# A clear between two scatters of the key phase, and statistics last in the normalized projections of a GNN kernel

## The reference, cut to what matters

```
h = max(layernorm(x), 0); x = x + GAT(h, 3 rounds, 1 head)      # L0
h = max(layernorm(x), 0); x = x + RGCN(h, 4 bases, edge types)  # L1
h = max(layernorm(x), 0); x = x + GAT(h, 1 round, 8 heads)      # L2
h = max(layernorm(x), 0); x = x + edge_conv(h)                  # L3
```

## Time and profile before

| | |
|---|---|
| median of three runs | 3939.06 us |
| profiled execution | 3923.35 us, its span 3921.4 us |
| busy: TensorE, DVE, ACT, POOL | 58%, 58%, 41%, 55% of the span |
| key phase | to 271 us, POOL's scatters from 57.4 to 187 us |
| p0 | first statistics 1310.2 us, last residual ends at 1456.4 us |
| p4 | first statistics 2649.2 us, last residual ends at 2864.3 us |

### The profile page before, as it was taken

The page is one execution under the profiler, slowest core; times in us unless marked ns, Lnnn a source line. Parts: engine busy times, 40 slices in busy tenths (PEclk is TensorE's granted clock), DMA queues, the critical chain, the costliest instruction groups (busy, mean ns, idle before and its releaser), DMA issues. The chain is left out here.

```text
span 3921.4 us, 53964 instructions
## 1 busy us (share of the span) xinstructions
PE 2263.7 (58%) x12833; PEld 1777.4 (45%) x12833; DVE 2282.0 (58%) x8009; ACT 1610.7 (41%) x3565; POOL 2157.8 (55%) x2121
## 2 busy tenths in 40 slices
PE   1035899999898565465565567754526443344333
PEld 1023676676677554364464444434425332233222
DVE  4154999999898785334345378866575333333233
ACT  0005999999997573223323322324411222122100
POOL 3618765575564332581185255546500588888755
PEclk9998999999999786577577588887756666666665
DMA  2140122332231454651663733333304333333253
GB/s 64 27 181 20 44 90 87 100 103 87 87 92 39 133 157 116 161 139 42 186 174 87 203 95 99 87 98 81 90 16 118 109 74 64 75 74 65 51 145 117
DMA packets 569029, 380.48 MB, mean 97 GB/s; under 512 B 51389, under 2 KB 511942, under 8 KB 568386
## 3 DMA queue, kind: packets, MB, share of 16 engines
q1 hardware_dynamic: 510050, 329.99, 28.7%
q0 software_dynamic: 56000, 46.29, 6.4%
q10 hardware_dynamic: 2720, 1.23, 0.2%
HBM read 249.08 MB, written 153.32 MB: 103 GB/s over the span
## 5 line engine op out<-in xcount | busy, mean ns | idle before, releaser
L1309 POOL DMA_INDIRECT p_a<-t_d,k_map_ix x300 | 309.1, 1030 | 291.3 <-DMA p_a<-t_d 241.1
L807 POOL TENSOR_TENSOR a_rs<-a_ve,w_neg_half 128x16 f32<-128x16 f32 x113 | 330.1, 2922 | 241.7 <-DVE a_ve L743 227.7
L833 ACT ACTIVATE a_nr<-a_xb,a_nm,a_rs 128x128 f32<-128x128 f32 x882 | 369.9, 487 | 26.1 <-POOL a_nm L809 26.1
L2064 POOL DMA_INDIRECT e_a<-t_d,e_ix x200 | 210.4, 1052 | 277.1 <-DMA e_a<-t_s 219.2
L895 PE MATMUL a_ps<-w_ident,a_nr 128*128 128x128 f32 x1568 | 245.6, 280 | 128.8 <-DVE a_xb L754 47.3
L903 PE MATMUL a_ps<-a_ht,w_aug 128*128 128x512 f32 x588 | 312.7, 616 | 2.4 <-DVE a_ht L710 2.4
L895 PEld LDWEIGHTS a_ps<-w_ident,a_nr 128*128 128x128 f32 x1568 | 179.9, 143 | 277.0 <-issue 244.5
L1431 PE MATMUL p_pm<-w_aug,p_ht 128*128 128x130 f32 (+1 forms) x1600 | 277.1, 343 | 7.6 <-ACT p_ht L1392 3.8
L710 DVE TENSOR_TENSOR a_ht<-a_ps,a_ht 128x512 f32<-128x512 f32 x294 | 201.5, 686 | 134.7 <-ACT a_ps L848 111.0
L1431 PEld LDWEIGHTS p_pm<-w_aug,p_ht 128*128 128x128 f32 x1600 | 261.4, 250 | 21.4 <-ACT p_ht L1392 11.9
L1789 PE MATMUL c_pq<-layer_src,c_sel 128*128 (+1 forms) x800 | 194.3, 420 | 124.7 <-ACT c_sel L1760 72.2
(11 more groups left out here) (358 smaller groups left out, 6449.0 us busy)
## 6 DMA issues: line engine op xcount, KB each, us to landing
t_s<-p_a SPq DMA_DIRECT2D x100, 256.0 KB
c_a<-t_d SPq DMA_DIRECT2D x100, 256.0 KB
t_d<-c_a SPq DMA_DIRECT2D x100, 256.0 KB
a_xa<-in_x SPq DMA_DIRECT2D x98, 256.0 KB
out<-a_xb SPq DMA_DIRECT2D x98, 256.0 KB, 2.0
p_a<-t_s SPq DMA_DIRECT2D x75, 256.0 KB
p_a<-t_d SPq DMA_DIRECT2D x75, 256.0 KB
t_acc<-q_zt SPq DMA_DIRECT2D x3, 2171.5 KB
```

The source lines that it names most:

```text
L807: nc.gpsimd.tensor_tensor(RS[:, z, :], VE[:, z, :], w["neg_half"][:, None, 0:J].to_broadcast([P, LNS, J]), ALU.pow).then_inc(s_rstd.sem, 1)
L833: last = nc.scalar.activation(NR[k][:, T.at(NORM[k], 2), cols(j)], normed_rows(T, k)[:, cols(j)], ACT.Identity, bias=NM[:, T.at(1, SHORT), ...
L1309: eng.indirect_dma_start(out=A[:, g, SRC, j, :], out_offset=None, in_=t[f"d{r}"], in_offset=bass.IndirectOffsetOnAxis(ap=k["map_ix"][:, b ...
L2064: eng.indirect_dma_start(out=A[:, g, side, j, :], out_offset=None, in_=t[f"d{r}"], in_offset=bass.IndirectOffsetOnAxis(ap=IX[:, g, what, j ...
```

## The change

In `keys` POOL clears a 128x256 tile behind every scatter, and waits before each clear for the one before, as `project` does behind its gathers. In `project` DVE's turn n becomes, for p0: residual of n - 4, hold of n - 3, statistics of n; for p4: hold of n - 3, residual of n - 3, statistics of n, so that p4 has 28 turns in place of 29. For p1 and p2 the list comes out as it was.

```diff
         M1 = sb("m1", [P, T], I32)
+        IDLE, s_idle = sb("idle", [P, 256]), sem("idle")
...
             for c in range(T):
                 eng.indirect_dma_start(out=t["maps"], out_offset=bass.IndirectOffsetOnAxis(ap=M1[:, c:c + 1], axis=0),
                                        in_=ID[:, c:c + 1], in_offset=None, bounds_check=NODES * WORDS - 1, oob_is_err=False).then_inc(s_map1, 16)
+                if c:
+                    eng.wait_ge(s_idle, c)
+                nc.gpsimd.memset(IDLE[:, :], 0.0).then_inc(s_idle, 1)
             eng.wait_ge(s_map1, 16 * T)
...
-            holds, residuals = (3, 4) if norm else (0, 1)
+            holds = 3 if norm else 0
+            residuals = holds if normed else holds + 1
             for n in range(BLOCKS + residuals):
+                if not normed and 0 <= n - residuals:
+                    residual(n - residuals)
+                if 0 <= n - holds < BLOCKS:
+                    hold(n - holds)
+                if normed and 0 <= n - residuals:
+                    residual(n - residuals)
                 if norm and n <= BLOCKS:
                     if n < BLOCKS:
                         there(eng, n)
                     mo.turn(eng, lambda m: A[:, n % RING, m // J, m % J, :], n, BLOCKS - 1)
-                if 0 <= n - residuals:
-                    residual(n - residuals)
-                if 0 <= n - holds < BLOCKS:
-                    hold(n - holds)
```

## The result

The changed kernel took 4091.85 us (median of 4 runs, 4089.26 to 4093.16) against 3940.16 us (4 runs): ratio 1.039, 95% interval 1.0365 to 1.0417. It is slower by 152 us; 4100 us were forecast. The profiled execution took 4089.26 us, span 4087.1 us. The table is read from one shift or scatter to the next in the two traces; lines of the changed kernel stand 1 to 7 higher than those of before.

What follows compares the result with a forecast made beforehand. DVE's waits among dense scatters bound the key phase, DVE p0; p4 also waited for gathers. 3923.35 - 60 (clears) + 141 (p0) + 91 (p4) = 4095, named as 4100 us; range 4030 to 4160 for 8 in 10.

Steps and rivals of the forecast that it cites:

- part one: Key phase: clears take DVE's waits away, POOL becomes the bound; phase ends at 211 in place of 271, -60 us.
- Rival 1: Key phase: the clear does not release DVE, +15 us in place of -60, 4170 us in all; chance 0.10.
- something between TensorE and DVE: Key phase: dense scatters hold it up; DVE waited 103.8 us in seven waits at line 447; resource not named.
- The order in p0 and p4: Projections: DVE's new order makes the loop serial, 11.6 us a turn in p0, 12.3 in p4: +141 and +91 us.
- the link that the prediction named: p0 and p4: ACT copies b only after its norm of b + 1, which needs the shift of b + 1.
- the slow clock: p0: TensorE at 1.2 GHz, product 3.67 us, turn 11.71; nearly that was taken, 11.6.
- The last blocks of p0: End of p0: two chains of 8.0 and some 7 us, 23 in place of 14.5, so +8.5 us.
- ACT's squash and DVE's residual of an older block fit inside the chain: p0's turn: a step that adds no time for them to the 11.6 us chain.
- DVE idle some 6 us a turn before the hold, for TensorE: Sign of being right in p0 and p4: idle before line 1346, released by TensorE's line 1431, turns of 11 to 13 us.
- Rivals 2 and 3: rival 2 has its own line; 3: one projection escapes by overlooked slack, 3954 or 4004 us, chance 0.05.
- rival 2: p4: products ready when DVE asks, earlier loads count; 6.0 us a turn, -56, 3807 us in all; chance 0.06.

Runs made afterwards that it cites:

- e1: Kernel before plus the change's key-phase clears alone, old order in p0 and p4: 3856.99 us, ratio 1.0047.
- e2: Kernel before plus the change's order in `project` alone, no clears in the key phase: 4045.49 us, ratio 1.0539.
- e5: Kernel before, no clears; each key-phase scatter waits until the scatter two before it has landed: 3933.91 us, one timed run.
- f1: Changed kernel, but in p0 and p4 ACT copies b right behind its norm, TensorE multiplies b right behind its transposes: 3939.32 us, ratio 0.9991.
- e3: Kernel before plus key-phase clears, statistics first; in p4 the residual of n - 3 right behind its hold: 3813.82 us, ratio 0.9929.
- h1: Changed kernel with f1's lists, p0's squash ahead of the norm, no key-phase clears, line 447 read ahead of the narrow write: 3901.46 us, one run.
- h3: Kernel before, narrow tile written by subtracting two tiles, and a 256-column clear behind each last-phase scatter: 3941.24 us, ratio 0.9969.
- k2: Kernel before with 256-column clears behind every fourth key-phase scatter and every last-phase scatter, h1's p0, f2's p4: 3868.82 us, ratio 0.9808.
- f2: Kernel before plus 8-column key-phase clears; p4 with e3's order and f1's prompt copy and product: 3868.14 us, ratio 0.981.

## Why the prediction was right, and where it was off

**The clears.** Right in kind for the condition in which the kernel before was traced: the waits of the earlier trace rows went, and POOL became the bound. Three sizes made -52 of -60: the scatters began 0.4 us later, the pitch was 1.51 us and not 1.49 (99 x 0.02 = 2 us), and from the last scatter's end (208.50) to the next phase 10.4 us passed, where 5 were taken. What was not seen is that the waits may be absent: then part one costs 16 us (e1), and the whole change, by the product of e1's and e2's ratios an estimate of 1.059, would be 5.9% slower. Rival 1 priced the wait that isn't freed; this is a wait that was never there. The forecast rested on one trace, and nothing in it said so.

The Trainium skill ("SBUF — State Buffer", Who interferes with whom) says that a DVE instruction with at most one SBUF input, outside the two-port modes, does not contend with GpSimd. The trace agrees so far as it goes: line 447 was not itself held up, it began 0.22 us after its signal was there (next paragraph). The step from there, in rival 1, to a wait that no clear takes away was wrong: slower scatters took it away with a clear (the changed kernel) and without one (e5).

**What comes late is TensorE's signal.** The trace also holds the times at which semaphores were raised; the views print only who raised them. In the earlier trace rows TensorE's last matmul is over at 147.11 us, its semaphore is raised at 165.45, and line 447 begins at 165.67. In an untroubled block the matmul is over at 201.50, the semaphore is raised at 201.51 and line 447 begins at 201.73. The 0.22 us is the same in all seven late blocks. So DVE takes its turn as promptly as ever, and what the prediction called "something between TensorE and DVE" lies before the semaphore's rise. The earlier trace rows shows the same: transposes over at 3800.35, semaphore raised at 3808.37, DVE at 3808.39.

**The order in p0 and p4.** The mechanism was right: DVE's own list makes the loop serial, one chain from a shift to the next. f1 takes out the link that the prediction named (ACT copies b only behind the norm of b + 1) and p4 goes from 12.0 to 6.2 us a turn. The turns came out at 11.09 in place of 11.6 and 12.00 in place of 12.3. In p0 I had taken nearly the slow clock; the granted clock was 0.65 of full, between its two levels, and the 22 products took 2.5 to 3.7 us, 3.09 on average, where 11.6 stands for nearly 3.67. The last blocks of p0 added 6.1 us and not 8.5. In these windows of p0 and p4 (window and its length, then busy us of TensorE's matmuls, its weight loads, DVE, ACT and POOL, then the granted clock, DMA share and GB/s) no engine is busy half of the time:

```profile
1265.00:1533.00 268.00, 126.42 (x600) 110.66 (x600) 125.32 (x757) 116.74 (x275) 49.99 (x50) 0.65 0.35 88
2735.00:3027.00 292.00, 132.46 (x600) 116.77 (x600) 126.52 (x759) 103.63 (x250) 118.19 (x178) 0.70 0.22 60
```

**The step that was wrong** is the sentence "ACT's squash and DVE's residual of an older block fit inside the chain". They fit, but hold DVE for 99.4 of its 131 us of idle time there, and alone they still kept p0 at 10.33 us a turn (f1). So one of the forecast's signs was missed in p0: DVE idle some 6 us a turn before the hold, for TensorE. It idled 4.7 us before the residual, for ACT, and 1.4 before the holds. The sum was safe only because the two chains run side by side and the product's is the longer by some 1.4 us, which the prediction hadn't worked out: that part was luck.

**Rivals 2 and 3** had no part in it: no product was ready when DVE asked, and neither projection escaped. But rival 2's promise was real: with the slack kept, the earlier stores are worth 43 us (e3).

**The rest.** p1 and p2 lie in the stretch between p0's last residual and p4's first shift, 1199.8 us before and 1202.5 after; the 6.8 us of the table are spread over three such stretches (1.4, 2.7, 2.6) with unchanged code, and e1's was 1202.5 too.

**Open.** Why TensorE's semaphore is raised late is not settled. DVE's signal to TensorE is prompt in the same blocks (TensorE, idle for 20.83 us in the earlier trace rows, began at 145.24, 0.05 us after DVE's write of its operand, 144.71 + 0.48). The delay stays with the wait for TensorE wherever that stands (h1), whatever the instruction before it (h3). At 3941 it goes with how fast the scatters come. One every 1.30 us (before) gave 104 us of waits, 1.38 (k2) 103 us, 1.42 (f2) 82 us, 1.51 (long clears) and 1.84 (e5) none above 0.6 us. A pause and a rate were never varied apart.

At 3841 one scatter every 1.33 us gave no wait at all, and a second thing differs there. The four traces at 3841 hold some 57,200 raised semaphores each, the ten others 38,100 to 42,400. The 100 scatters raise theirs 1600 times: e2's trace holds 1598 of them, that of the kernel before 204, that of the changed kernel 1145. So where the signal is late, the trace itself lacks many of these events. Whether both have one cause, and whether taking the trace has a part in it, no run tests.

## What to carry to other kernels

Before an engine's work is put ahead of other work in its list, follow every input of what now stands in front back to the last thing that this engine itself must do for it; if that is the previous turn, the loop has become serial, and its turn is the length of the chain. Two chains can start at the same point, and taking out one shows the other. A gain that rests on an odd wait in one trace should be checked in another group of runs, and on another chip if there is one, before it is kept: here the same code had 104 us of it or none. And a late start behind a wait has two halves, the signal and the engine that takes it; where the trace has the time of the signal, look which of them is late.

## What the runs showed of the hardware

The same program took 3841 us in one group of runs (19 runs, 3825.61 to 3850.57) and 3940 to 3951 in the others. The clock is not the reason: the granted clock was 0.782 to 0.790 in these 19 runs and 0.784 to 0.795 in those of the same kernel beside f1 to k2. Nearly all of the distance (95 of 99 us) is in two phases with scatters close behind one another. In the key phase they are 0.98 us long with 0.30 us between, and there TensorE's semaphore is raised up to 18.6 us after its last matmul is over (kernel before), while DVE starts 0.22 us after the rise. One scatter every 1.51 us (a clear of 128x256, 0.34 us, behind each, which leaves 0.49 us between two) takes the delay away, and so does waiting for landed scatters (one every 1.84 us).
